# Feed-forward part of a two-stage layer: Newton steps of the norms on GpSimd, norms in pieces, a shared last tile, a halved last block

## Chip, cores and metric

The kernel runs on one core of one Trainium2 chip, in float32. The metric is the device time of one execution in microseconds. The time before is the median of three runs.

## What is computed

A layer of two parts on `x` with 4 sequences of 1024 tokens and 256 features (T = 4096 rows):

```python
x = x + layernorm(attn(layernorm(x)))     # gated delta rule, 32 value heads, chunks of 64
x = x + layernorm(ffn(layernorm(x)))
def ffn(x):                               # weights are lut[idx], 16 entries
    h = silu(x @ lut[gate_idx].T) * (x @ lut[up_idx].T)     # 688 wide
    return h @ lut[down_idx].T
def layernorm(x):
    return (x - mean(x)) / sqrt(var(x) + 1e-5)
```

## The kernel before

The main part (attention) takes the first 4200 us. It is one unrolled loop over 64 units of work on all engines, and it also builds the feed-forward weights from the table: for each of 16 slices of `WC` = 268 columns, VectorE compares the indices with each of the 16 entries (L896) and GpSimd adds up the results (L1438); the slices go to DRAM as `wtd`. A barrier (L1875 to L1897) ends it. A is then the sum of the attention's output, in SBUF.

The feed-forward part has five functions, one for each engine's queue: `ffn_sp`, `ffn_dve`, `ffn_pe`, `ffn_act`, and after the change `ffn_pool`. The order of the work on an engine is the order in which its function writes it, and semaphores hold the engines together. It goes in 8 blocks `b` of 512 tokens (4 rows of tiles of 128 tokens, `js`).

- **Norms (VectorE).** Three norms for each block: norm 0 of the attention's output, added to x (L1619, result in A); norm 1 of that, into xs, as input of the matmuls; norm 2 of the feed-forward output F, added to A (L1640). Each is `stats` (4 bn_stats, 4 bn_aggr, the variance, and `newton` for 1/sqrt: a seed and 3 rounds of 4 small instructions, L97 to L106) and `norm_out` (4 instructions, L1575).
- **Tiles of the hidden width.** 688 = 5 x 128 + 48, so FT = 6 tiles t. `gate_up(b, t)` on TensorE (L1667) has a group of matmuls for gate and one for up, into two PSUM banks: strip and emit for even t, ml and mr for odd t. Weights are stationary, 512 tokens move; the last tile has 48 weight columns. ScalarE takes silu of gate (`sg`, L1712), VectorE multiplies it with up (`gate`, L1602, result in hb).
- **Down.** `down(b, n)` for 4 groups n of 128 tokens (L1677), two into bank kv, two into bank qa; ScalarE copies them to F (`fo`, L1716).
- **TensorE's order** in a block b: gate_up 0, 1, 2; down(b-1) 0, 1 (kv); gate_up 3, 4, 5; transposes of xs for block b+1 (pp, L1655); down(b-1) 2, 3 (qa). gate_up(b, t) waits until the multiply two tiles earlier is done (`s["h"]` at i-1 with i = 6b + t), because that frees its banks; down waits for all six of its block.
- **VectorE's order** in step j (block b = j-1): gate 0; stats and out of norm 0 of block j; gate 1; the add; gate 2; stats and out of norm 1 of block j; gate 3, 4; stats of norm 2 of block j-2, which waits for its F; gate 5; out and add of norm 2.

Of the kernel before, what the change touches and what calls it, by code (L numbers as in the profile page):

```python
# [8 lines left out]
I32 = mybir.dt.int32  # L9
ALU = mybir.AluOpType  # L10
# [1547 lines left out]
def norm_stats(nc, dv, s, st, mv, var, rstd, tn, src, j, k):

    v = nc.vector  # L1560
    js = slice(4 * j, 4 * j + 4)
    for n in range(4):
        v.bn_stats(st[:, 4 * j + n, :], src[:, 4 * j + n, :]).then_inc(s["bs"], 1)  # L1563
    for n in range(4):
        dv.wait_ge(s["bs"], NT + 4 * k + n + 1)
        v.bn_aggr(mv[:, 4 * j + n, :], st[:, 4 * j + n, :]).then_inc(s["mv"], 1)  # L1566
    dv.wait_ge(s["mv"], NT + 4 * k + 4)
    v.tensor_scalar(var[:, js], mv[:, js, 1], 1e-5, None, ALU.add).then_inc(s["rsq"], 1)
    newton(dv, s["rsq"], 14 * (k + 2) + 1, var[:, js], rstd[:, js], tn[:, js])
    dv.wait_ge(s["rsq"], 14 * (k + 3))  # L1570


def norm_out(nc, s, mv, rstd, src, fin, j):
    for n in range(4 * j, 4 * j + 4):
        nc.vector.tensor_scalar(fin[:, n, :], src[:, n, :], mv[:, n, 0:1], rstd[:, n:n + 1],  # L1575
                                ALU.subtract, ALU.mult).then_inc(s["xn"], 1)


def norms_before(i, j):

    if i < 2:
        return 2 * j + i + max(0, j - 2)
    return 2 * min(j + 3, 8) + j


def ffn_dve(nc, s, g, f, bk):
    dv, v = Engine(nc.vector), nc.vector

    def stats(i, j, src):
        norm_stats(nc, dv, s, f.st[:, i], f.mv[:, i], f.var[:, i], f.rstd[:, i], f.tn[:, i], src, j,  # L1590
                   norms_before(i, j))

    def out(i, j, src, fin):
        norm_out(nc, s, f.mv[:, i], f.rstd[:, i], src, fin, j)

    def gate(b, t):
        i = b * FT + t
        rows = 128 if t < FT - 1 else FR
        dv.wait_ge(s["sg"], i + 1)
        dv.wait_ge(s["gu"], 2 * i + 2)  # L1600
        dv.wait_ge(s["dp"], 4 * (b - 1))
        v.tensor_tensor(f.hb[b % 2][0:rows, t, :], bk.all[3 + 2 * (i % 2)][0:rows, :], f.sg[i % 2][0:rows, :],  # L1602
                        ALU.mult).then_inc(s["h"], 1)

    for j in range(10):
        gates = [(j - 1, t) for t in range(FT)] if 1 <= j <= 8 else []
        if gates:
            gate(j - 1, 0)
        if j < 8:
            js = slice(4 * j, 4 * j + 4)  # L1610
            if j < 4:
                dv.wait_ge(s["da%d" % (j // 2)], 16)
            stats(0, j, f.A)
            out(0, j, f.A, f.A)
            if gates:
                gate(j - 1, 1)
            dv.wait_ge(s["xn"], NT + 4 * norms_before(0, j) + 4)
            dv.wait_ge(s[f"x{j // 2}"], 32)
            v.tensor_tensor(f.A[:, js, :], f.A[:, js, :], f.xs[:, js, :], ALU.add).then_inc(s["x1f"], 1)  # L1619
            if gates:  # L1620
                gate(j - 1, 2)
            dv.wait_ge(s["x1f"], j + 1)
            stats(1, j, f.A)
            out(1, j, f.A, f.xs)
        elif gates:
            gate(j - 1, 1)
            gate(j - 1, 2)
        if gates:
            gate(j - 1, 3)
            gate(j - 1, 4)  # L1630
        if j >= 2:
            b = j - 2
            js = slice(4 * b, 4 * b + 4)
            dv.wait_ge(s["fo"], 2 * b + 2)
            stats(2, b, f.F)
            if gates:
                gate(j - 1, 5)
            out(2, b, f.F, f.F)
            dv.wait_ge(s["xn"], NT + 4 * norms_before(2, b) + 4)
            v.tensor_tensor(f.F[:, js, :], f.F[:, js, :], f.A[:, js, :], ALU.add).then_inc(s["o"], 1)  # L1640
        elif gates:
            gate(j - 1, 5)
# [125 lines left out]


def program(nc, x, wqkv, wz, wo, convw, wba, dtb, alog, normw, lut, widx,  # L1770
            c_f32, c_mask, c_reset, c_u0, out):
    with ExitStack() as ctx:
# [104 lines left out]
        with ExitStack() as tmp:  # L1877
            f = Bag()
            f.A = g.A
            f.xnT = alloc(tmp, "fxnT", [128, 2, T])  # L1880
# [4 lines left out]
            f.var = alloc(tmp, "var2", [128, 3, NT])
            f.rstd = alloc(tmp, "rstd2", [128, 3, NT])
            f.tn = alloc(tmp, "tn2", [128, 3, NT])
# [3 lines left out]
            f.gu = f.ws[:, 0:4 * INTER].rearrange("p (w h n) -> p w h n", w=2, h=2)  # L1891
            f.dn = f.ws[:, 4 * INTER:].rearrange("p (t n) -> p t n", t=FT)
# [69 lines left out]
```

## Time and profile before

| | us |
|---|---|
| median of 3 runs | 4530.6 (4528.2 to 4533.37) |
| profiled execution | 4533.44 |
| its span | 4531.0 |
| main part, to the barrier | about 4201 |
| feed-forward part | about 330 |
| mean granted TensorE clock | 0.985 |

The profile shows one execution. PE is TensorE, DVE VectorE, ACT ScalarE, POOL GpSimd, SP the queue that issues most transfers. A line number is that of the code above; Newton instructions have the lines of their helper. In a timeline, equal instructions in a row are merged, xcount of them, and an idle time ahead of them stands in brackets with what ended it. Matmuls of float32 show two records each.

### The profile page before, as it was taken

Reading aid. Unit: us, or ns where it says so; the run is one execution under the profiler, and the core shown is the slowest. Engines: PE = TensorE matmul, PEld = TensorE weight load, DVE = VectorE, ACT = ScalarE, POOL = GpSimd, SP = SyncE. Lnnn points to the kernel's source line nnn. Section 1 sums busy time; section 2 is a strip of 40 time slices with the busy share of each in tenths; the row PEclk is TensorE's granted clock in tenths of the full one; section 3 lists DMA queues with packets and bytes.
Section 4 is the critical chain, followed back from the end, with each engine's and each line's share of the span. In section 5 each row is a group of like instructions: output and inputs, shape, how many; then the busy total and the mean of one; then the engine's idle time right before and its main releaser. Section 6 shows DMA issues by size and latency. Waiting matters only on the chain. (4 is left out here: it accounts for less than half of the span.)

```text
span 4531.0 us, 93023 instructions
## 1 busy us (share of the span) xinstructions
PE 4297.6 (95%) x30676; PEld 3229.5 (71%) x30676; DVE 3523.2 (78%) x8064; ACT 2981.9 (66%) x6124; POOL 2987.7 (66%) x8711
## 2 busy tenths in 40 slices
PE   5899999999999999999999999999999999998898
PEld 2577777777777777777777777777777777776444
DVE  6688888888888888878888788878888888885554
ACT  3577777777777767766777767766777767774111
POOL 1677777777777777777777777777777777774000
PEclk7899999999999999999999999999999999999899
DMA  4222222222222222222222222222232222210200
GB/s 133 56 65 60 67 67 46 67 59 68 67 57 65 60 67 59 55 71 64 67 67 55 64 63 59 62 68 60 67 75 47 69 58 69 64 36 20 71 14 19
DMA packets 592240, 275.17 MB, mean 61 GB/s; under 512 B 464400, under 2 KB 548880, under 8 KB 582544
## 3 DMA queue, kind: packets, MB, share of 16 engines
q1 hardware_dynamic: 591040, 266.62, 23.9%
q8 instruction: 244, 4.00, 0.4%
q0 software_dynamic: 720, 2.62, 0.3%
q14 instruction: 236, 1.93, 0.1%
HBM read 221.84 MB, written 47.28 MB: 59 GB/s over the span
## 5 line engine op out<-in xcount | busy, mean ns | idle before, releaser
L714 DVE SCALAR_TENSOR_TENSOR CV<-pp,CW,CV 128x1023 f32<-128x1023 f32 (+2 forms) x768 | 980.3, 1276 | 33.1 <-ACT CV L1076 21.8
L339 PE MATMUL pp<-A,W 128*128 128x512 f32 x2048 | 970.4, 602 | 30.1 <-DVE CV L714 18.8
L1373 POOL TENSOR_TENSOR UL<-UL,TM 128x126 f32<-128x126 f32 (+22 forms) x1984 | 743.4, 375 | 155.4
L1370 POOL TENSOR_TENSOR TM<-UL,XL 128x126 f32<-128x126 f32 (+22 forms) x1984 | 708.5, 357 | 147.2 <-issue 12.6
L339 PEld LDWEIGHTS pp<-A,W 128*128 128x128 f32 x2048 | 377.7, 193 | 338.8 <-issue 307.2
L1172 ACT ACTIVATE QE<-qa,TAB 128x128 f32<-128x128 f32 x1024 | 318.2, 362 | 407.9 <-PE qa L468 407.8
L834 DVE SCALAR_TENSOR_TENSOR St<-St,TAB,kv 128x128 f32<-128x128 f32 x1024 | 309.0, 343 | 325.0 <-PE kv L487 317.2
L1183 ACT ACTIVATE VS<-qa,EB 128x128 f32<-128x128 f32 x1024 | 319.1, 364 | 300.5 <-PE qa L478 294.7
L510 PE MATMUL emit<-Wz,A 128*128 128x256 f32 x2048 | 492.0, 383 | 4.3 <-DVE A L885 4.1
L531 PE MATMUL emit<-Wo,NTr 128*128 128x256 f32 x2048 | 493.7, 384 | 1.3 <-ACT NTr L1216 1.3
L1076 ACT ACTIVATE CV<-pp,CW 128x1024 f32<-128x1024 f32 x256 | 285.0, 1113 | 231.2 <-PE pp L339 231.2
L531 PEld LDWEIGHTS emit<-Wo,NTr 128*128 128x128 f32 x2048 | 375.9, 191 | 55.2 <-ACT NTr L1216 11.2
L510 PEld LDWEIGHTS emit<-Wz,A 128*128 128x128 f32 x2048 | 370.0, 191 | 48.0 <-DVE A L885 5.8
L820 DVE SCALAR_TENSOR_TENSOR R<-kv,TAB,V 128x128 f32<-128x128 f32 x1024 | 309.9, 344 | 119.0 <-PE kv L458 112.8
L478 PEld LDWEIGHTS qa<-R,N 128*128 128x128 f32 x2048 | 299.1, 191 | 140.7 <-issue 122.5
L458 PE MATMUL kv<-St,QK 128*128 128x256 f32 x1024 | 336.2, 410 | 43.5 <-DVE St L834 43.0
L871 DVE SCALAR_TENSOR_TENSOR CO<-CO,ty,emit 128x128 f32<-128x128 f32 x1024 | 286.9, 343 | 102.3 <-POOL ty L1357 96.5
L478 PE MATMUL qa<-R,N 128*128 128x128 f32 x2048 | 317.9, 278 | 24.7 <-issue 18.9
L487 PE MATMUL kv<-VS,K 128*128 128x256 f32 x1024 | 326.8, 401 | 5.8 <-ACT VS L1183 5.7
L1135 ACT ACTIVATE GB<-GB,AB 128x128 f32<-128x128 f32 x1024 | 328.6, 398 | 2.3
L748 DVE SCALAR_TENSOR_TENSOR X<-strip,RHO,GB 128x256 f32<-128x256 f32 x512 | 223.9, 479 | 135.7 <-ACT GB L1135 130.8
L497 PEld LDWEIGHTS qa<-VN,AT 128*128 128x128 f32 x2048 | 304.6, 191 | 23.3
(220 smaller groups left out, 9242.3 us busy)
## 6 DMA issues: line engine op xcount, KB each, us to landing
GB<-gcd SPq DMA_DIRECT2D x64, 1024.0 KB, 4.9
W<-wqkv SPq DMA_DIRECT2D x256, 128.0 KB, 3.7
XL<-xb SPq DMA_DIRECT2D x128, 256.0 KB, 3.9
UL<-c_u SPq DMA_DIRECT2D x64, 256.0 KB, 2.9
xb<-X SPq DMA_DIRECT2D x512, 32.0 KB, 1.7
Wz<-wz SPq DMA_DIRECT2D x64, 256.0 KB, 2.8
ub<-UL SPq DMA_DIRECT2D x128, 128.0 KB, 2.9
N<-ub SPq DMA_DIRECT2D x256, 64.0 KB, 2.3
```

Of the source, the lines that this page charges most:

```text
L339: ins = t.matmul(bk.pp[:, 512 * h:512 * h + 512], m.W[:, c, k, :], m.xnT[:, w // KH % 2, c, 512 * h:512 * h + 512], start=c == 0, stop=c == 1)
L458: t.matmul(bk.kv[:, 0:256], m.QK[:, 3 + w % 3, c * 128:(c + 1) * 128], sf, start=True, stop=True).then_inc(s["ks"], 1)
L478: ins = t.matmul(bk.qa[:, 256 + 128 * r:384 + 128 * r], m.N1[w % 2][:, 2 * c + r, :], m.R[k % 2][:, r, :], start=True, stop=True)
L487: t.matmul(bk.kv[:, 0:256], m.K[w % 3][:, c, :], m.VS[:].rearrange("p r d -> p (r d)"), start=True, stop=True).then_inc(s["sup"], 1)
L510: ins = t.matmul(bk.out[:, c * 256:(c + 1) * 256], m.xnT[:, w // KH % 2, h, t0:t0 + 128], m.Wz[:, w % 2, h, :], start=h == 0, stop=h == 1)
L531: ins = t.matmul(bk.out[:, c * 256:(c + 1) * 256], m.NTr[:, 2 * c + r, :], m.Wo[:, w % 2, r, :], start=r == 0, stop=r == 1)
L714: v.scalar_tensor_tensor(m.CV[:, t, d:S], bk.pp[:, 0:S - d], m.CW[:, w % KH, t, 3 - d:4 - d], m.CV[:, t, d:S], ALU.mult, ALU.add).then_inc ...
L1135: ins = a.activation(row, row, ACT.Exp, bias=m.AB[w % 2][:, 2 * q + c, r:r + 1])
L1172: ins = a.activation(m.QE[:, r, :], bk.qa[:, r * 128:(r + 1) * 128], ACT.Copy, scale=m.TAB[w % 2][:, EG, c, r:r + 1])
L1183: ins = a.activation(m.VS[:, r, :], bk.qa[:, 256 + r * 128:384 + r * 128], ACT.Copy, scale=m.EB[w % 2][:, c, r:r + 1])
L1370: gp.tensor_tensor(m.TM[:, 0:a, 0:b], m.UL[:, 0:a, k:k + 1].to_broadcast([128, a, b]), m.XL[:, k, k + 1:32].unsqueeze(1).to_broadcast([128 ...
L1373: gp.tensor_tensor(m.UL[:, 0:a, k + 1:32], m.UL[:, 0:a, k + 1:32], m.TM[:, 0:a, 0:b], ALU.subtract).then_inc(s["sub"], 1)
```

## The change

The Newton rounds of all norms go from VectorE to GpSimd (`newton_pool` with 12 small instructions, as the main part has it), but for the last block's norm 2; VectorE still computes the seed. VectorE's order is written anew: norms 0 and 1 are two blocks ahead of the gates, `stats`, `out` with its add, and the second norm stand between different gates, and norm 2 of a block is spread over the block two later. Gate and up of the last tile share one group of matmuls with 112 weight columns (48 gate, 16 zero, 48 up), one PSUM bank, partitions 0 to 47 and 64 to 111; down then contracts over all 128 rows of the last tile, of which GpSimd has set the unused ones to zero. In the diff, s1(j) is `stats(0, j)`, o1(j) `out(0, j)` with the add of x; s2, o2 are norm 1; s3(b), o3(b) norm 2 of block b; root(i, j) on GpSimd waits for the seed of norm i, block j, and runs `newton_pool`. The last block's norm 2 is worked off by `last(k)` in two halves of 2 x 128 tokens, with `newton` on VectorE, and so is its transfer. WC grows from 268 to 270.

```diff
-FR = INTER - 128 * (FT - 1)
-WCOLS = 4 * INTER + FT * HID
+FM = 128 * (FT - 1)
+FR = INTER - FM
+HC = 2 * FM + 64 + FR
+GUC = 2 * HC
+WCOLS = GUC + FT * HID
...
 def ffn_dve(nc, s, g, f, bk):
...
     def stats(i, j, src):
-        norm_stats(nc, dv, s, f.st[:, i], f.mv[:, i], f.var[:, i], f.rstd[:, i], f.tn[:, i], src, j,
-                   norms_before(i, j))
+        js = slice(4 * j, 4 * j + 4)
+        for n in range(4 * j, 4 * j + 4):
+            v.bn_stats(f.st[:, i, n, :], src[:, n, :]).then_inc(s[f"nb{i}"], 1)
+        dv.wait_ge(s[f"nb{i}"], 4 * j + 4)
+        for n in range(4 * j, 4 * j + 4):
+            v.bn_aggr(f.mv[:, i, n, :], f.st[:, i, n, :]).then_inc(s[f"nm{i}"], 1)
+        dv.wait_ge(s[f"nm{i}"], 4 * j + 4)
+        v.tensor_scalar(f.var[:, i, js], f.mv[:, i, js, 1], 1e-5, None, ALU.add).then_inc(s[f"nv{i}"], 1)
+        dv.wait_ge(s[f"nv{i}"], 2 * j + 1)
+        v.tensor_scalar(f.rstd[:, i, js].bitcast(I32), f.var[:, i, js].bitcast(I32), -0.5, MAGIC, ALU.mult,
+                        ALU.add).then_inc(s[f"nv{i}"], 1)
     def out(i, j, src, fin):
+        dv.wait_ge(s[f"np{i}"], 12 * j + 12)
+        for n in range(4 * j, 4 * j + 4):
+            v.tensor_scalar(fin[:, n, :], src[:, n, :], f.mv[:, i, n, 0:1], f.rstd[:, i, n:n + 1],
+                            ALU.subtract, ALU.mult).then_inc(s[f"nx{i}"], 1)
+...
     def gate(b, t):
+        dv.wait_ge(s["gu"], GUN * b + min(2 * t + 2, GUN))
...
+            dv.wait_ge(s["hz"], 2)
+            v.tensor_tensor(f.hb[b % 2][64:64 + FR, t, :], bk.all[2 + 2 * (i % 2)][64:64 + FR, :],
+                            f.sg[i % 2][64:64 + FR, :], ALU.mult).then_inc(s["h"], 1)
+    def last(k):
+        n0, i0 = NT - 4 + 2 * k, 15 * k
+        js = slice(n0, n0 + 2)
+        dv.wait_ge(s["fo"], 15 + k)
...
+        newton(dv, s["nl"], 14 * k + 1, f.var[:, 2, js], f.rstd[:, 2, js], f.tn[:, js])
...
+    s1(0)
+    s1(1)
+    o1(0)
+    s2(0)
+    o1(1)
+    s2(1)
+    o2(0)
+    o2(1)
+    for b in range(8):
+        gate(b, 0)
+        if b < 6:
+            s1(b + 2)
+        gate(b, 1)
+        if b >= 2:
+            s3(b - 2)
+        gate(b, 2)
+        if b < 6:
+            o1(b + 2)
+            s2(b + 2)
+        gate(b, 3)
+        if b >= 2:
+            o3(b - 2)
+        gate(b, 4)
+        if b < 6:
+            o2(b + 2)
+        gate(b, 5)
+    s3(6)
+    o3(6)
+    last(0)
+    last(1)
+def ffn_pool(nc, s, f):
+    for hb in f.hb:
+        gp.memset(hb[:, FT - 1, :], 0.0).then_inc(s["hz"], 1)
+    root(0, 0)
+    root(0, 1)
+    root(1, 0)
+    root(1, 1)
+    for b in range(8):
+        if b < 6:
+            root(0, b + 2)
+        if b >= 2:
+            root(2, b - 2)
+        if b < 6:
+            root(1, b + 2)
+    root(2, 6)
...
     def gate_up(b, t):
+        if t == FT - 1:
+            for h in range(2):
+                ins = nc.tensor.matmul(bk.all[2 + 2 * (i % 2)][0:64 + FR, :], f.gu[:, h, 2 * FM:HC],
+                                       f.xnT[:, h, b * 512:(b + 1) * 512], start=h == 0, stop=h == 1)
+            ins.then_inc(s["gu"], 1)
+            return
...
     def down(b, n):
...
-                                   f.hb[b % 2][0:rows, t, n * 128:(n + 1) * 128], f.dn[0:rows, t, :],
+                                   f.hb[b % 2][:, t, n * 128:(n + 1) * 128], f.dn[:, t, :],
```

## Rows read from the trace of the kernel before

**Rows 1.** Page, section 1: busy us, share of the span, instructions.
```profile
PE 4297.6 (95%) x30676; PEld 3229.5 (71%) x30676; DVE 3523.2 (78%) x8064; ACT 2981.9 (66%) x6124; POOL 2987.7 (66%) x8711
```

**Rows 2.** Windows between the blocks' first matmuls: length, engines' busy us, clock, DMA share.
```profile
core 0: us, PE busy (x) PEld busy (x) DVE busy (x) ACT busy (x) POOL busy (x), PEclk, DMA share, GB/s
4242.90:4276.60 33.70, 33.65 (x104) 17.69 (x104) 14.97 (x58) 5.27 (x9) 0.00 (x0) 1.00 0.00 0
4276.60:4312.80 36.20, 33.92 (x105) 17.61 (x104) 21.97 (x86) 5.87 (x10) 0.00 (x0) 1.00 0.05 15
4312.80:4350.80 38.00, 35.71 (x105) 18.20 (x105) 22.08 (x86) 5.87 (x10) 0.00 (x0) 0.96 0.04 14
...
4462.80:4500.00 37.20, 34.92 (x97) 17.36 (x96) 10.56 (x33) 4.78 (x8) 0.00 (x0) 0.95 0.04 14
```

**Rows 3.** Waits, 4250 to 4531 us: us in total, times, longest.
```profile
PE ml L1667 <- DVE hb L1602: 13.7, 6, 2.3
```

**Rows 4.** Timeline of PE, blocks 1 to 3: start, us, what, [idle before].
```profile
4282.61 1.98 PE L1667 MATMUL ml<-fxnT,ws 128*128 128x512 f32 x4 [2.28 <-DVE hb L1602]
...
4302.51 1.92 PE L1667 MATMUL ml<-fxnT,ws 128*48 128x512 f32 x4
4304.26 1.88 PE L1667 MATMUL mr<-fxnT,ws 128*48 128x512 f32 x4
...
4318.85 3.68 PE L1667 MATMUL ml<-fxnT,ws 128*128 128x512 f32 x4 [2.29 <-DVE hb L1602]
```

**Rows 5.** Timeline of DVE, block 6.
```profile
4463.62 1.41 DVE L1563 BATCH_NORM_STATS2 st<-F 128x6 f32<-128x256 f32 x4 [10.22 <-ACT F L1716]
...
4465.54 0.17 DVE L97 TENSOR_SCALAR rstd<-var 128x4 int32<-128x4 int32 x1
...
4468.13 0.68 DVE L1602 TENSOR_TENSOR hb<-mr,sg 48x512 f32<-48x512 f32 x1
4468.73 1.36 DVE L1575 TENSOR_SCALAR F<-F,mv,rstd 128x256 f32<-128x256 f32 x4
```

**Rows 6.** Timelines of DVE (first row) and PE at the start of the part.
```profile
4201.78 1.41 DVE L1563 BATCH_NORM_STATS2 st<-A 128x6 f32<-128x256 f32 x4 [0.33 <-PEq L1875]
...
4214.27 1.97 PE L1655 MATMUL pp<-cf,xs 128*128 128x128 f32 x8 [13.54 <-DVE xs L1575]
4217.02 3.42 PE L1667 MATMUL strip<-fxnT,ws 128*128 128x512 f32 x4 [0.78 <-ACT fxnT L1704]
...
4229.41 1.98 PE L1667 MATMUL ml<-fxnT,ws 128*128 128x512 f32 x4 [0.39 <-DVE hb L1602]
...
4237.55 1.92 PE L1667 MATMUL ml<-fxnT,ws 128*48 128x512 f32 x4 [1.00 <-DVE hb L1602]
```

**Rows 7.** GpSimd: timelines of POOL and DVE, and one Newton line (ns min/median/max).
```profile
36.22 1.80 POOL L1442 MEMSET N<- 128x2048 f32 x1 [35.78 <-PE kv L546]
...
68.92 1.13 POOL L1355 TENSOR_SCALAR tk<-tk 128x8 f32<-128x8 f32 x1
...
68.78 2.35 DVE L757 TENSOR_TENSOR GB<-GB,cm 128x1024 f32<-128x1024 f32 x2
...
L1355 POOL TENSOR_SCALAR tk<-tk x192: 195/203/1131, 67.8 to 4071.9; 128x8 f32<-128x8 f32 x192
...
4190.70 0.16 DVE L861 TENSOR_SCALAR ty<-tv 128x4 int32<-128x4 int32 x1
4194.34 1.12 DVE L871 SCALAR_TENSOR_TENSOR CO<-CO,ty,emit 128x128 f32<-128x128 f32 x4 [3.47 <-POOL ty L1357]
```

**Rows 8.** Timelines of PE (first row) and DVE at the end.
```profile
4505.96 8.06 PE L1677 MATMUL kv<-ws,hb 128*128 128x256 f32 x24 [5.91 <-DVE hb L1602]
...
4520.66 1.41 DVE L1563 BATCH_NORM_STATS2 st<-F 128x6 f32<-128x256 f32 x4 [12.20 <-ACT F L1716]
...
4526.58 1.23 DVE L1640 TENSOR_TENSOR F<-F,A 128x1024 f32<-128x1024 f32 x1
```

**Rows 9.** One line's durations (ns min/median/max), and DMA issues (KB, us to landing).
```profile
L1438 POOL TENSOR_TENSOR wd<-wd,wv x240: 748/755/761, 98.6 to 4098.3; 128x268 f32<-128x268 f32 x120
...
y<-F SPq DMA_DIRECT2D x8, 512.0 KB, 2.9
```

More of the change, by code:

```diff
@@ L22 @@
 FT = (INTER + 127) // 128
-FR = INTER - 128 * (FT - 1)
-WCOLS = 4 * INTER + FT * HID
+FM = 128 * (FT - 1)
[3 more added lines that the diff above has]
+WCOLS = GUC + FT * HID
 WC = WCOLS // KH
-GUK = -(-4 * INTER // WC)
+GUK = -(-GUC // WC)
+GUN = 2 * FT - 1
 MAGIC = 1597463007.0
@@ L1555, in main_pool @@
     return start, loop
[L1558 to L1583, printed above, removed]
 def ffn_dve(nc, s, g, f, bk):
@@ new lines, in s1, with o1, s2, o2 @@
+    def s1(j):
+        if j < 4:
+            dv.wait_ge(s["da%d" % (j // 2)], 16)
+        stats(0, j, f.A)
+    def o1(j):
+        js = slice(4 * j, 4 * j + 4)
+        out(0, j, f.A, f.A)
+        dv.wait_ge(s["nx0"], 4 * j + 4)
+        dv.wait_ge(s[f"x{j // 2}"], 32)
+        v.tensor_tensor(f.A[:, js, :], f.A[:, js, :], f.xs[:, js, :], ALU.add).then_inc(s["x1f"], 1)
+    def s2(j):
+        dv.wait_ge(s["x1f"], j + 1)
+        stats(1, j, f.A)
+    def o2(j):
+        out(1, j, f.A, f.xs)
@@ L1596, in gate, with s3, o3 @@
+    def s3(b):
+        dv.wait_ge(s["fo"], 2 * b + 2)
+        stats(2, b, f.F)
+    def o3(b):
+        js = slice(4 * b, 4 * b + 4)
+        out(2, b, f.F, f.F)
+        dv.wait_ge(s["nx2"], 4 * b + 4)
+        v.tensor_tensor(f.F[:, js, :], f.F[:, js, :], f.A[:, js, :], ALU.add).then_inc(s["o"], 1)
     def gate(b, t):
         i = b * FT + t
-        rows = 128 if t < FT - 1 else FR
         dv.wait_ge(s["sg"], i + 1)
-        dv.wait_ge(s["gu"], 2 * i + 2)
+        dv.wait_ge(s["gu"], GUN * b + min(2 * t + 2, GUN))
@@ L1601, in gate @@
         dv.wait_ge(s["dp"], 4 * (b - 1))
[L1602 to L1642, printed above, removed]
@@ new lines, in gate @@
+        if t < FT - 1:
+            v.tensor_tensor(f.hb[b % 2][:, t, :], bk.all[3 + 2 * (i % 2)][:, :], f.sg[i % 2][:, :],
+                            ALU.mult).then_inc(s["h"], 1)
+        else:
+            dv.wait_ge(s["hz"], 2)
[5 more added lines that the diff above has]
+        dv.wait_ge(s["fo"], 15 + k)
+        for n in range(n0, n0 + 2):
+            v.bn_stats(f.st[:, 2, n, :], f.F[:, n, :]).then_inc(s["nb2"], 1)
+        dv.wait_ge(s["nb2"], n0 + 2)
+        for n in range(n0, n0 + 2):
+            v.bn_aggr(f.mv[:, 2, n, :], f.st[:, 2, n, :]).then_inc(s["nm2"], 1)
+        dv.wait_ge(s["nm2"], n0 + 2)
+        v.tensor_scalar(f.var[:, 2, js], f.mv[:, 2, js, 1], 1e-5, None, ALU.add).then_inc(s["nl"], 1)
+        newton(dv, s["nl"], 14 * k + 1, f.var[:, 2, js], f.rstd[:, 2, js], f.tn[:, js])
+        dv.wait_ge(s["nl"], 14 * k + 14)
+        for n in range(n0, n0 + 2):
+            v.tensor_scalar(f.F[:, n, :], f.F[:, n, :], f.mv[:, 2, n, 0:1], f.rstd[:, 2, n:n + 1],
+                            ALU.subtract, ALU.mult).then_inc(s["nx2"], 1)
+        dv.wait_ge(s["nx2"], n0 + 2)
+        v.tensor_tensor(f.F[:, js, :], f.F[:, js, :], f.A[:, js, :], ALU.add).then_inc(s["o"], 1)
@@ new lines, in ffn_dve, with root @@
+    last(1)
+def ffn_pool(nc, s, f):
+    po, gp = Engine(nc.gpsimd), nc.gpsimd
+    def root(i, j):
+        js = slice(4 * j, 4 * j + 4)
+        po.wait_ge(s[f"nv{i}"], 2 * j + 2)
+        newton_pool(po, s[f"np{i}"], 12 * j, f.var[:, i, js], f.rstd[:, i, js], f.tp[:, i, js])
+    for hb in f.hb:
[12 more added lines that the diff above has]
+    root(2, 6)
@@ L1660, in gate_up @@
         i = b * FT + t
-        rows = 128 if t < FT - 1 else FR
         pe.wait_ge(s["ws"], 16)
@@ L1664, in gate_up @@
         pe.wait_ge(s["h"], i - 1)
+        if t == FT - 1:
[4 more added lines that the diff above has]
+            return
         for w in range(2):
             for h in range(2):
-                ins = nc.tensor.matmul(bk.all[2 + 2 * (i % 2) + w][0:rows, :], f.gu[:, w, h, t * 128:t * 128 + rows],
+                ins = nc.tensor.matmul(bk.all[2 + 2 * (i % 2) + w][:, :], f.gu[:, h, w * FM + t * 128:w * FM + t * 128 + 128],
                                        f.xnT[:, h, b * 512:(b + 1) * 512], start=h == 0, stop=h == 1)
@@ L1675, in down @@
         for t in range(FT):
-            rows = 128 if t < FT - 1 else FR
             ins = nc.tensor.matmul(bk.all[6 + n // 2][:, (n % 2) * 256:(n % 2) * 256 + 256],
-                                   f.hb[b % 2][0:rows, t, n * 128:(n + 1) * 128], f.dn[0:rows, t, :],
+                                   f.hb[b % 2][:, t, n * 128:(n + 1) * 128], f.dn[:, t, :],
                                    start=t == 0, stop=t == FT - 1)
@@ L1708, in sg @@
         i = b * FT + t
-        rows = 128 if t < FT - 1 else FR
-        ac.wait_ge(s["gu"], 2 * i + 1)
+        ac.wait_ge(s["gu"], GUN * b + min(2 * t + 1, GUN))
         ac.wait_ge(s["h"], i - 1)
-        a.activation(f.sg[i % 2][0:rows, :], bk.all[2 + 2 * (i % 2)][0:rows, :], ACT.Silu).then_inc(s["sg"], 1)
+        if t < FT - 1:
+            a.activation(f.sg[i % 2][:, :], bk.all[2 + 2 * (i % 2)][:, :], ACT.Silu).then_inc(s["sg"], 1)
+        else:
+            a.activation(f.sg[i % 2][64:64 + FR, :], bk.all[2 + 2 * (i % 2)][0:FR, :], ACT.Silu).then_inc(s["sg"], 1)
     def fo(b, k):
@@ L1751, in ffn_sp @@
     xs(3)
-    for b in range(8):
+    for b in range(9):
         sp.wait_ge(s["o"], b + 1)
-        nc.sync.dma_start(dr.out.rearrange("(n p) h -> p n h", p=128)[:, 4 * b:4 * b + 4, :],
-                          f.F[:, 4 * b:4 * b + 4, :]).then_inc(s["out"], 16)
-    sp.wait_ge(s["out"], 128)
+        ns = slice(4 * b, 4 * b + 4) if b < 7 else slice(14 + 2 * b, 16 + 2 * b)
+        nc.sync.dma_start(dr.out.rearrange("(n p) h -> p n h", p=128)[:, ns, :], f.F[:, ns, :]).then_inc(s["out"], 16)
+    sp.wait_ge(s["out"], 144)
 SEMS = ("cf", "x0", "x1", "x2", "x3", "cb", "wb", "l127", "hd", "al", "reset", "xnw", "g3a", "tabw",
@@ L1886, in program @@
             f.rstd = alloc(tmp, "rstd2", [128, 3, NT])
-            f.tn = alloc(tmp, "tn2", [128, 3, NT])
+            f.tn = alloc(tmp, "tn2", [128, NT])
+            f.tp = alloc(tmp, "tp2", [128, 3, NT])
             f.ws = alloc(tmp, "ws", [128, WCOLS])
@@ L1890, in program @@
             f.sg = [alloc(tmp, f"sg{i}", [128, 512]) for i in range(2)]
[L1891 to L1892 removed]
+            f.gu = f.ws[:, 0:GUC].rearrange("p (h n) -> p h n", h=2)
+            f.dn = f.ws[:, GUC:].rearrange("p (t n) -> p t n", t=FT)
             ffn_sp(nc, s, f, dr)
@@ L1896, in program @@
             ffn_act(nc, s, g, f, bk)
+            ffn_pool(nc, s, f)
             nc.all_engine_barrier()
@@ L1931 @@
     ba = np.stack([a["L0_attn_W_b"], a["L0_attn_W_a"]]).reshape(2, 32, 2, 128).transpose(3, 2, 0, 1)
-    gu = [a[n].reshape(INTER, 2, 128).transpose(2, 1, 0).reshape(128, 2 * INTER)
-          for n in ("L0_ffn_gate_idx", "L0_ffn_up_idx")]
-    dt = a["L0_ffn_down_idx"].T
-    dt = np.concatenate([dt, dt[:FT * 128 - INTER]], 0).reshape(FT, 128, HID).transpose(1, 0, 2).reshape(128, FT * HID)
-    wi = np.concatenate(gu + [dt], 1).reshape(128, KH, WC).transpose(1, 0, 2)
+    gi, ui = (a[n].reshape(INTER, 2, 128).transpose(2, 1, 0) for n in ("L0_ffn_gate_idx", "L0_ffn_up_idx"))
+    gu = np.zeros((128, 2, HC), gi.dtype)
+    gu[:, :, 0:FM], gu[:, :, FM:2 * FM] = gi[:, :, 0:FM], ui[:, :, 0:FM]
+    gu[:, :, 2 * FM:2 * FM + FR], gu[:, :, 2 * FM + 64:HC] = gi[:, :, FM:], ui[:, :, FM:]
+    di = a["L0_ffn_down_idx"].T
+    dt = np.zeros((FT * 128, HID), di.dtype)
+    dt[0:FM], dt[FM + 64:FM + 64 + FR] = di[0:FM], di[FM:]
+    dt = dt.reshape(FT, 128, HID).transpose(1, 0, 2).reshape(128, FT * HID)
+    wi = np.concatenate([gu.reshape(128, GUC), dt], 1).reshape(128, KH, WC).transpose(1, 0, 2)
     cf, mask, reset, u0 = consts()
```

3 lines of the change are left out of this document (1 added, 2 removed), and 3 rows, old and new, of the table SEMS.

## The prediction, made before the changed kernel ran

> **What bounds the kernel now.** I read the page first, then the windows, then the waits, then the timeline of each engine around the waits. TensorE is busy 95% of the span [rows 1], so a change is worth what it takes from TensorE's work or from TensorE's idle time. The change touches only the feed-forward part, which begins where VectorE reads A after the barrier (4201.78 us), so I cut the windows at the first matmul of each block b, the one of gate_up(b, 0) [rows 2]. Block 1 (4242.9 to 4276.6) has PE busy for 33.65 of 33.70 us: that is a block with no wait. Blocks 2 to 6 take 36.2 or 37.9 us with the same matmuls. The list of waits names the reason: TensorE waits six times, 13.7 us in all, for hb on the ml bank [rows 3], and once, 5.91 us, ahead of the last down-projection [rows 8]. In the timeline [rows 4] the first pause is at gate_up(b, 1), 2.28 us, whose bank is freed by gate(b-1, 5). In the next such place (block 6) VectorE runs that multiply at 4468.13, though its tile was computed before the block began, since the `stats(2, ...)` of the third norm stands ahead of it: this waits 10.22 us for the F of the last down-projection, starts at 4463.62 and takes 4.5 us, of which 13 Newton instructions are 2.6 [rows 5]. The pause of 5.91 us is the same multiply again [rows 8].
>
> **The start.** Today VectorE needs 12.5 us from 4201.78 until TensorE's first transpose at 4214.27 [rows 6]. The new order puts more ahead of it. A `stats` up to the seed's start takes 4465.54 - 4463.62 = 1.92 us and the seed 0.2, so 2.1 without Newton steps; an `out` is 1.4 [rows 5], the add 1.23 [rows 8]. A chain on GpSimd is 12 instructions spaced 0.28 us: from VectorE's seed at 4190.70 to its next reader at 4194.34 it is 3.64 us, so 3.4 from GpSimd's first to VectorE's next [rows 7]. From zero: s1(0) to 2.1, s1(1) to 4.25; GpSimd has chain (0,0) from 2.2 to 5.6; o1(0) 5.6 to 8.2; s2(0) to 10.35; o1(1), whose chain ended at 9.0, to 13.0; s2(1) to 15.15, while chain (1,0) ends at 13.7; o2(0) at 15.15, the transpose 0.79 later: 15.95. The two memsets ahead of the chains are 512 columns each; 2048 took 1.80 us [rows 7], and GpSimd has 2.2 us for them. I add 0.1 to 0.2 for what follows, so the start costs **+3.6**.
>
> GpSimd and VectorE disturb each other: a Newton instruction with a median of 203 ns took 1131 ns at 68.92 us, while VectorE ran two adds of 128x1024 [rows 7]. One chain of each tensor meets such an add of 1.22 us in the start, which lets it end at 10.2 and 15.1 instead of 9.0 and 13.9, each just before it is read (10.35, 15.15). The Trainium skill, page "SBUF — State Buffer", section "Who interferes with whom", says that a VectorE instruction with two SBUF inputs contends with a GpSimd instruction that reads SBUF, and that the second to issue fully blocks until the first has finished; the rows agree. By that rule the start would be up to 0.3 us longer than without it, and bn_stats, with one SBUF input, would not disturb GpSimd.
>
> **Block 0.** Today 25.93 us from its first matmul to block 1's. VectorE's order costs pauses of 0.39 and 1.00 us [rows 6] and a refill of about 0.16 behind each, my estimate from a group of 1.98 behind a pause [rows 4] against 1.82 to 1.88. In the new order gate(0,3) is done 18.1 us after the first matmul, when t5 could start at 18.7. The last tile is the next term: gate and up of 48 columns are two groups today, the second 4304.26 - 4302.51 = 1.75 us behind the first. A group with 48 weight columns takes as long as one with 128 (1.92 against 1.98 behind a pause) [rows 4], so one with 112 will too: one group saved, **1.75 us a block**. Block 0: -1.7 - 1.75 = **-3.45**. Start and block 0 cancel: block 1 begins near 4243 again.
>
> **Blocks 1 to 6.** From block 1's first matmul to block 7's it is 4462.8 - 4242.9 = 219.9 us [rows 2]. No pause stays if each multiply is done in time. From a block's start, with 33.7 - 1.75 = 31.95 us of matmuls: gate0 4.5; s1 to 6.6; gate1 7.9; s3 to 10.0 (its F is there since 0.7); gate2 11.3; o1 and its add to 14.0; s2 to 16.1; gate3 when t3 ends, 20.5; o3 to 23.2; gate4 23.9; o2 to 25.3; gate5 26.4. TensorE needs gate5 at 35.4: 9 us to spare. GpSimd has chain s1 from 6.4 to 9.9 (read at 11.3), s3 to 13.3 or, lengthened by o1's add, 14.5 (read at 20.5), s2 from 16.0 to 19.4 (read at 23.9). So 6 x 31.95 = 191.6, **-28.3**. Of this 10.5 is the shared tile; the rest is the pauses, 2.55 each, and the clock: after the pause at 4318.85 the ml group took 3.68 instead of 1.98 [rows 4], a loss of 1.7 in each of the four blocks of 37.9 and 37.2 us, whose mean granted clock is 0.95 or 0.96: a stretch behind the pause at 1.2 instead of 2.4 GHz [rows 2]. With no pause ahead I expect 1.00 throughout, as in block 1.
>
> **Block 7 and the last down-projection.** Block 7 takes 37.2 to the end of its last group at 4505.96 - 5.91 = 4500.05; less 2.55, 1.69 and 1.75 it is 31.2, **-6.0**. Then TensorE waits 5.9 us for gate(7,5) and restarts slowly, kv 8.06 us [rows 8] for the 5.9 that 24 such matmuls take at full clock elsewhere in the timeline; the new gate(7,5) runs before that point: **-8.05**. Behind it, with D the end of down(6): s3(6) is the new next-late thing. F at D+0.7, seed D+2.7, chain to D+6.3, o3(6) to D+8.95. F of the first half has been ready since D+6.65, so it waits 2.3 us. A half costs, from the durations of the whole [rows 5, 8]: stats 0.75, aggregate 0.25, var 0.2, 13 Newton instructions 2.6, out 0.75, add 0.65: 5.2. Two run one after the other: D+19.35, where today's tail at full clock would be D+19.7: **-0.4**, not the 2.0 that half the elementwise work would suggest. The last transfer halves (landing at 2.9 us [rows 9]; between no gain and 1 us): I take **-0.3**.
>
> **The main part** does the same instructions, with 270 columns instead of 268 for building the weights. 240 adds on GpSimd at 755 ns [rows 9], 0.75% longer, are 1.4 us beside TensorE, VectorE's steps for them less; bounds -3 to +4, taken at 0. Extra last-tile rows in `down` cost nothing: a matmul's time follows its 256 columns; zero rows only fill it. ScalarE's and VectorE's last tile keep 512 columns.
>
> **Sum:** 3.6 - 3.45 - 28.3 - 6.0 - 8.05 - 0.4 - 0.3 = -42.9. Span 4531.0 to 4488.1; the profiled run was 4533.44, so 4490.5 for it. The median of the three runs is 4530.6, which gives **4488** (4487.7).
>
> **Rivals.**
> (1) Newton chains twice as long. The instruction of 1131 ns speaks for it, the median of 203 ns over 192 of its kind against it [rows 7]. The blocks don't notice (o2 would start at 26.8, gate5 28.9, needed at 35.4), but the start has three chains in a row (+7.4) and the tail one (+3.4): 4499. Chance 0.08.
> (2) Slower: one mechanism, GpSimd's instructions held by VectorE at 1.1 us each, as the longest row, so 13.2 us a chain. Three chains a block are then 39.6 us, more than TensorE's 31.95, and GpSimd sets the pace: 7 x 7.65 = 54, the start 29, the tail 10, together +93 on 4488: 4581. It becomes slower than before from about 0.93 us an instruction on. Against it: VectorE's two-input adds cover only 2.5 us of a block. Chance 0.02.
> (3) The last tile saves nothing, because a group with 112 weight columns costs what the two did: 8 x 1.75 back, 4502. The equal times of 48 and 128 columns speak against it. Chance 0.03.
> (4) The main part, 4200 us long, moves by more than 4 us, since its buffers and semaphores shift: either way, 4478 or 4500. No row speaks for it. Chance 0.10.
> (5) The pauses go but TensorE is granted 1.2 GHz somewhere else for one stretch or more, 1.7 us each, or some pause of the waits' kind remains: 4490 to 4497. Chance 0.12.
> The forecast case has 0.65, with a range of its own of 4484 to 4493. The range that holds 8 in 10 takes in (5), the bounds above and part of (1) and (4): 4480 to 4499. A measurement here can tell about 0.2%, 9 us. All cases but (2) and a far outlier of (4) are faster by more: faster 0.95, same 0.02, slower 0.03.
>
> **What would show it.** Right: windows of 32 us between strip's first matmuls with the clock at 1.00, no wait of TensorE for hb beyond the start, the first transpose near 4217.8, kv following qa without a gap, the end of the last F near 4485. Wrong: `o1` or `o2` waiting for GpSimd on VectorE for microseconds within a block; Newton instructions with a mean well above 0.3 us; L1667's last group above 2 us; a start of the feed-forward part that isn't at 4201.8.

## The result

The changed kernel takes 4473.9 us (median of 4 runs, 4472.6 to 4475.1) against 4531.8 us beside it: ratio 0.9875, 95% interval 0.9863 to 0.9887, or 57.9 us less. Forecast were 4488 us, in a range of 4480 to 4499. The profiled execution has a span of 4470.8 us, 60.2 less than the one of before. In a later series the same two kernels stood at 4476.3 and 4529.6 (ratio 0.9881, 0.9865 to 0.9898).

The windows of the changed kernel, cut at the same places as [rows 2]; the columns are those of [rows 2].

```profile
4196.20:4215.00 18.80, 1.99 (x9) 1.62 (x9) 14.79 (x54) 1.19 (x2) 13.02 (x50) 0.50 1.01 327
4215.00:4238.80 23.80, 22.89 (x53) 10.23 (x53) 12.80 (x38) 4.66 (x8) 4.84 (x25) 0.88 0.18 56
4238.80:4268.90 30.10, 30.10 (x100) 18.26 (x101) 12.80 (x36) 5.25 (x9) 4.73 (x24) 1.00 0.00 0
4268.90:4299.00 30.10, 30.10 (x102) 18.23 (x101) 16.65 (x50) 5.85 (x10) 8.22 (x36) 1.00 0.06 19
...
4419.60:4449.00 29.40, 29.40 (x94) 17.59 (x93) 8.70 (x21) 4.77 (x8) 2.36 (x12) 1.00 0.05 18
4449.00:4470.80 21.80, 10.36 (x49) 8.77 (x47) 13.99 (x57) 1.79 (x3) 2.36 (x12) 0.82 0.14 48
```

Blocks 1 to 7 have no pause, PE is busy in all of each window and the clock is granted at 1.00, as forecast. But a block takes 30.1 us and not 31.95: TensorE's own work is 3.6 us shorter than in the block without a pause in [rows 2], where one group of 1.75 was counted on. The timeline of PE in block 2 of the changed kernel, to be read beside [rows 4]:

```profile
4277.58 1.88 PE L1728 MATMUL emit<-fxnT,ws 128*128 128x512 f32 x4
4279.30 5.34 PE L1737 MATMUL kv<-ws,hb 128*128 128x256 f32 x24
4284.48 1.88 PE L1728 MATMUL ml<-fxnT,ws 128*128 128x512 f32 x4
...
4291.35 1.88 PE L1722 MATMUL ml<-fxnT,ws 128*112 128x512 f32 x4
4293.06 1.04 PE L1711 MATMUL pp<-cf,xs 128*128 128x128 f32 x8
4293.94 5.34 PE L1737 MATMUL qa<-ws,hb 128*128 128x256 f32 x24
```

From the start of kv to the next group it is 4284.48 - 4279.30 = 5.18 us. The same 24 records took 5.86 in the kernel before.

Each part of the feed-forward stage, in us, read from the starts of these groups in the two traces:

| part | before | after | difference | forecast |
|---|---|---|---|---|
| first norm to first transpose | 12.49 | 16.03 | +3.54 | +3.6 |
| block 0, from its first matmul | 25.93 | 23.80 | -2.13 | -3.45 |
| blocks 1 to 6 | 219.93 | 180.82 | -39.11 | -28.3 |
| block 7 to the end of qa | 37.17 | 29.40 | -7.77 | -6.0 |
| from there to VectorE's end | 27.76 | 19.35 | -8.41 | -8.45 |
| to the end of the span | 3.19 | 2.45 | -0.74 | -0.3 |
| feed-forward part, with 2.75 ahead of block 0 | 329.2 | 274.6 | -54.6 | -42.9 |
| main part (start of the first norm) | 4201.8 | 4196.2 | -5.6 | 0 |

### The profile page after: what moved, and what is told of

Same layout as the page of the kernel before. It is cut to its first block and busy times, and to the rows that moved or that the text cites. A ratio compares the mean times of both kernels' runs of the same rounds, so it can differ in the third digit from the quotient of the medians.

```text
span 4470.8 us, 92997 instructions
## 1 busy us (share of the span) xinstructions
PE 4252.6 (95%) x30644; PEld 3229.0 (72%) x30644; DVE 3483.3 (78%) x7803; ACT 2976.3 (67%) x6124; POOL 3039.3 (68%) x8989
```

## The experiments

**Why is a block shorter than forecast?** Theory A: a group of matmuls whose number of rows differs from its neighbours' costs TensorE extra. Theory B, the one of the prediction: only the columns count. Two kernels put the 48 rows back into the changed kernel, and take them out of the kernel before.

e1_down48, edit against the changed kernel:

```diff
         for t in range(FT):
+            rs = slice(0, 128) if t < FT - 1 else slice(64, 64 + FR)
...
-                                   f.hb[b % 2][:, t, n * 128:(n + 1) * 128], f.dn[:, t, :],
+                                   f.hb[b % 2][rs, t, n * 128:(n + 1) * 128], f.dn[rs, t, :],
```

> The changed kernel, but down's last tile contracts over its 48 rows (64 to 111) again instead of 128. Theory A (a group whose row count differs from its neighbours' costs TensorE extra at each change of shape): in the trace of before 24 records of down take 5.86 us from group to group, in that of after 5.18, so 0.34 for each of 32 groups n: +10.9 us, about 4485, and blocks of 31.5 us instead of 30.1. Theory B (a matmul follows its columns alone, as predicted): 0, 4474, and the missing time lies elsewhere.

e5_down128, edit against the kernel before (and the two memsets of hb's last tile on GpSimd, which the multiply waits for):

```diff
-            rows = 128 if t < FT - 1 else FR
...
-                                   f.hb[b % 2][0:rows, t, n * 128:(n + 1) * 128], f.dn[0:rows, t, :],
+                                   f.hb[b % 2][:, t, n * 128:(n + 1) * 128], f.dn[:, t, :],
```

> The kernel before, but down's last tile contracts over 128 rows, of which GpSimd has set 48 to 127 to zero; nothing else changed. Theory A: -10.9 us, about 4521, block 1 at 32.3 instead of 33.7 us. Theory B: no change, 4532. The pauses for the gate multiply stay at about 2.3 us in both.

Measured, with 4526.6 us for the kernel before beside them: e1 4480.4 us (4475.6 to 4485.2; ratio to before 0.9895, 0.9879 to 0.9912), its blocks 31.68 us, its feed-forward part 284.4. That is 9.8 more than the changed kernel's, and 10.8 more than the 273.6 of e12, the changed kernel again (below), whose block 0 took as long as e1's (22.8 us). e5 4510.8 (ratio 0.9968, 0.9955 to 0.9981), its block 1 32.22 us instead of 33.68, its feed-forward part 317.5 (-11.7), with pauses still there, of 2.48 us. Timelines of PE, block 2: e1, then e5.

```profile
4282.66 5.93 PE L1738 MATMUL kv<-ws,hb 128*128 128x256 f32 x24
```

```profile
4276.82 2.46 PE L1674 MATMUL ml<-fxnT,ws 128*128 128x512 f32 x4 [2.48 <-DVE hb L1603]
4285.49 5.34 PE L1683 MATMUL kv<-ws,hb 128*128 128x256 f32 x24
```

The duration of the 24 records goes to 5.93 with 48 rows in the new kernel and to 5.34 with 128 in the old one. Theory B falls: what 24 such records take goes with the rows of the last tile, in the new order and in the old. TensorE's weight loads show where it is lost, e1 first and then the changed kernel:

```profile
4297.97 2.03 PEld L1738 LDWEIGHTS qa<-ws,hb 128*128 128x128 f32 x10
4300.33 0.29 PEld L1738 LDWEIGHTS qa<-ws,hb 48*128 48x128 f32 x2 [0.33 <-issue]
4300.96 2.02 PEld L1738 LDWEIGHTS qa<-ws,hb 128*128 128x128 f32 x10 [0.33 <-issue]
```

```profile
4263.71 5.05 PEld L1737 LDWEIGHTS qa<-ws,hb 128*128 128x128 f32 x24
```

In e1 the weight load waits 0.33 us ahead of the first load of the other shape, on the way in and on the way out; in the changed kernel the 24 loads follow each other without a gap. Is it the change of shape, or are 48-row matmuls slow in themselves? e11_fewer_switches has as many 48-row matmuls as e1, but half as many changes of shape. What it has beyond e1's edit:

```diff
-        for t in range(FT):
+        order = [FT - 1] + list(range(FT - 1)) if n % 2 else list(range(FT))
+        for t in order:
...
-                                   start=t == 0, stop=t == FT - 1)
+                                   start=t == order[0], stop=t == order[-1])
```

> e1_down48 (down's last tile over 48 rows), but every second group n takes that tile first, so that two 48-row tiles stand next to each other and the shape changes half as often. Theory A1 (the change of shape costs): blocks of 30.9 instead of 31.68 us, half of the 1.56 comes back. Theory A2 (a matmul over 48 rows is slower in itself): 31.68 stays.

Measured in one execution (4477.7 us): blocks of 30.91 us. PEld and PE of e11:

```profile
4296.02 0.62 PEld L1739 LDWEIGHTS qa<-ws,hb 128*128 128x128 f32 x3
4296.97 0.73 PEld L1739 LDWEIGHTS qa<-ws,hb 48*128 48x128 f32 x4 [0.33 <-issue]
4298.03 2.02 PEld L1739 LDWEIGHTS qa<-ws,hb 128*128 128x128 f32 x10 [0.33 <-issue]
```

```profile
4279.69 5.74 PE L1739 MATMUL kv<-ws,hb 128*128 128x256 f32 x24
```

A block has 4 visits to the other shape in e1, 2 in e11 and none in the changed kernel: 31.68, 30.91, 30.12. Each visit costs 0.39 us (0.37 by e5's block 1 against that of before), and 48-row matmuls next to each other cost nothing more: A1. The Trainium skill, page "TensorEngine Tiling (Array Packing)", section "Key Properties", says that changing the tiling mode drains TensorE. It doesn't say that matmuls over 48 rows and over 128 rows are two modes. If they are, these runs agree with it, at 0.39 us for a change and the change back; that a drain is what costs the time isn't shown by them.

**How the gain divides.** e2_order is the changed kernel with the old last tile (`gate_up`, `sg`, `gate`, `down` and the weights' layout as before; no memset). e3_tile is the kernel before with only these pieces of the change.

> The changed kernel with the old last tile (two groups of 48 columns, down over 48 rows, 268 columns a slice): new order, Newton on GpSimd and halved last block alone. Theory A: the tile's part of the gain goes back, 8 x 1.75 for the group, 10.9 for down and 8 x 0.2 for the changes of shape around the last tile: 4474 + 26.5 = 4500. Theory B: 8 x 1.75 alone, 4488. The main part: if its 5.6 us earlier end is due to the 270 columns, VectorE's first norm is back at about 4202; if it is chance or due to something else, it stays where it is by chance.

> The kernel before with the shared last tile alone (270 columns a slice), old order, Newton on VectorE, last block whole. Theory A: 4532 - 26.5 = 4505, with the six pauses of about 2.3 us still there. Theory B: 4532 - 14 = 4518. If the 270 columns are what moves the main part, its norm starts at about 4196 and the time is 5 us less again.

Measured: e2 4494.6 us (ratio 0.9931, 0.9916 to 0.9946), feed-forward part 300.4, blocks 33.68. e3 4500.2 (ratio 0.9942, 0.9928 to 0.9957), feed-forward part 305.8. In e2's PE the blocks are just those that [rows 2] had without a pause (33.70), and no pause is left; in e3 all six pauses stand, at 2.49 us:

```profile
4262.80 1.92 PE L1714 MATMUL ml<-fxnT,ws 128*48 128x512 f32 x4
4264.56 1.88 PE L1714 MATMUL mr<-fxnT,ws 128*48 128x512 f32 x4
4266.37 1.09 PE L1702 MATMUL pp<-cf,xs 128*128 128x128 f32 x8
4267.30 5.93 PE L1724 MATMUL qa<-ws,hb 128*128 128x256 f32 x24
```

```profile
4272.11 2.46 PE L1686 MATMUL ml<-fxnT,ws 128*128 128x512 f32 x4 [2.49 <-DVE hb L1610]
...
4306.68 2.90 PE L1686 MATMUL ml<-fxnT,ws 128*128 128x512 f32 x4 [2.49 <-DVE hb L1610]
```

By the feed-forward parts, the new order with Newton on GpSimd and the halved end is worth 329.2 - 300.4 = 28.8 us, the tile on top of it 300.4 - 274.6 = 25.8; the tile alone, in the old order, 23.4. In a block the tile brings 33.68 - 30.12 = 3.56 us: 1.72 are the group saved, 1.56 the changes of shape in `down` (e1), and the rest, 0.28, those around the 48-column groups (1.76 us from the first to the second and 1.81 from that to pp, against 1.72 within a shape).

Sums of whole parts are less sharp than this. e9 (below) has the same feed-forward code as the kernel before, and its part took 332.5 us, 3.3 more: 1.6 in block 0 and 1.7 in blocks 1 to 6, where the clock fell behind four pauses instead of three. So the 28.8 could as well be 32, and 23.4 against 25.8 doesn't show that the tile brings less alone.

**What is GpSimd for?** e4_newton_dve keeps the new order and puts all Newton rounds back on VectorE (in `stats`, with `newton`; GpSimd has only the memsets).

> The changed kernel with all Newton rounds on VectorE, in the same new order. Theory: in a block VectorE has 3 x 2.4 us more, gate 3 then ends at about 22.5 us from the block's start, where TensorE wants it at 22.35, so 0 to 0.3 us a block; the start has three stats of 4.5 us and more in a row ahead of the first transpose: 24.2 instead of 16.0 us, +8.2; the end -0.8. Sum 4474 + 7.4 to 9.5 = 4481 to 4484. Rival (the move to GpSimd is what removes the pauses): pauses of 2 us come back in every block with the lower clock behind them, +20 us or more.

Measured: 4479.3 us (ratio 0.9896, 0.9881 to 0.9911), feed-forward part 285.0: +10.4. The first transpose is 24.21 us behind the first norm (24.2 expected), most blocks take 30.34 us against 30.12. No pause between the blocks comes back. Only block 0 has one, which I had not expected:

```profile
4243.52 1.97 PE L1703 MATMUL ml<-fxnT,ws 128*112 128x512 f32 x4 [1.78 <-DVE hb L1617]
```

So the rival falls: the order, in which no `stats` that waits for F stands ahead of gate 5, is enough to remove the pauses. GpSimd's part on top of it is 8.2 us at the start and 2 to 3 us in block 0 (25.87 us against 23.80, and 22.78 in e12).

The fourth case, the old order with Newton on GpSimd, was not run. There the 12 Newton instructions that stand between the seed and gate 5 [rows 5] would be gone from VectorE. They take 12 x 0.2 = 2.4 us, and the six pauses are 2.28: by this estimate the move alone could have removed these too, though of the pause of 5.91 us it would leave some 3.5. What is shown is that the order suffices, not that it is needed.

**The end: is halving worth anything?** e7_whole has the last block's third norm and its transfer in one piece:

```diff
-    last(0)
-    last(1)
+    last()
```

> The changed kernel with the last block's third norm in one piece. By the trace of after its last half begins at 4463.06, while F has been there since 4460.0: the two halves wait for each other. In one piece 7.15 us from 4460.05 on: VectorE ends 18.2 us behind the end of down(6) instead of 19.35, the transfer is 0.3 longer: -0.8 us. Rival (halving saves half of the elementwise work at the end): +2 us.

Measured: 4468.5 us (4463.0 to 4472.1; ratio 0.9868, 0.9853 to 0.9882), feed-forward part 274.0 (-0.6). VectorE ends 18.3 us behind the end of down(6), as expected, against 19.35 with halves. The timelines of VectorE at the end: the changed kernel, then e7.

```profile
4456.70 1.23 DVE L1611 TENSOR_TENSOR F<-F,A 128x1024 f32<-128x1024 f32 x1
4457.84 0.75 DVE L1631 BATCH_NORM_STATS2 st<-F 128x6 f32<-128x256 f32 x2
...
4463.06 0.74 DVE L1631 BATCH_NORM_STATS2 st<-F 128x6 f32<-128x256 f32 x2
...
4467.66 0.69 DVE L1643 TENSOR_TENSOR F<-F,A 128x512 f32<-128x512 f32 x1
```

```profile
4456.80 1.41 DVE L1630 BATCH_NORM_STATS2 st<-F 128x6 f32<-128x256 f32 x4 [2.10 <-ACT F L1776]
...
4462.85 1.22 DVE L1642 TENSOR_TENSOR F<-F,A 128x1024 f32<-128x1024 f32 x1
```

The first half doesn't start when its F is there (4454.8) but when o3(6) is done, and the second half waits for the first one's Newton steps. In one piece VectorE even idles for 2.10 us and is done earlier. The halved transfer gives back part of it: it lands after 2.1 us instead of 2.9. Of the 0.6 us this leaves 0.3 (1.05 less on VectorE, 0.78 more behind it); the other 0.3 is block 0's start, which scatters. The medians can't show so little, and they come from different series; it is the two traces that do.

**A better start?** The new order puts two blocks' norms ahead of the first transpose, at +3.54 us. e8_start_end takes block 0's norms first, with Newton on VectorE, and joins the end anew (s3(6) with Newton on VectorE, one Newton chain for both halves of the last block). The order of the start:

```diff
     s1(0)
-    s1(1)
     o1(0)
     s2(0)
+    o2(0)
+    s1(1)
     o1(1)
     s2(1)
-    o2(0)
     o2(1)
```

> The changed kernel with the start in the old order (s1(0), o1(0), s2(0), o2(0) first, their Newton rounds on VectorE) and a new end: s3(6) with Newton on VectorE, the last block's statistics in halves, one Newton chain for both, output in halves. The start costs 12.5 us instead of 16.0 to the first transpose (-3.5), and block 0's multiplies have 5 us of VectorE's norms of block 1 ahead of them, which is hidden as in before (TensorE's first gate is wanted at 5.2 us). The end: 17.5 us behind down(6) instead of 19.35 (-1.9). Sum 4474 - 5.4 = 4468.5. Rival: the 3.5 us come back, because the norms of block 1 now delay gate 0 of block 0: 4472.

e10_weave has e8's start and end, and interleaves the rest with block 0:

```diff
...
+    s1(1)
     o1(1)
+    gate(0, 0)
     s2(1)
-    o2(0)
+    gate(0, 1)
+    s1(2)
+    gate(0, 2)
     o2(1)
-    for b in range(8):
+    gate(0, 3)
+    o1(2)
+    gate(0, 4)
+    s2(2)
+    gate(0, 5)
+    for b in range(1, 8):
         gate(b, 0)
+        if b == 1:
+            o2(2)
...
```

> The start of e8_start_end (block 0's norms first, Newton on VectorE) and its end, but the norms of blocks 1 and 2 in pieces between the gates of block 0, so that gate(0,0) no longer has both norms of block 1 ahead of it. In e8_start_end TensorE waited 4.04 us for that gate and block 0 took 30.25 us for 23.8. Theory: no pause in block 0, which takes 23.5 to 25; first transpose 12.7 us behind the first norm; end 17.7 us behind down(6): feed-forward part 274.6 - 3.3 - 1.7 = 269.6 us. Rival (VectorE has too much to do in block 0, whatever the order): pauses of 1 to 3 us, 271 to 275.

> The changed kernel again, on the same chip as the two below. Its feed-forward part took 274.6 us from VectorE's first norm to the end of the span; it should do so again within 1.5 us, while the end of the main part may lie anywhere between 4190 and 4202, as in the ten traces so far. Median 4467 to 4474.

Measured: e8 4471.1 us (ratio 0.9874, 0.9858 to 0.9891), feed-forward part 276.1, 1.5 longer than the changed kernel's. The start and the end gained nearly what was expected (12.75 us to the first transpose for 12.5, VectorE's end 17.7 us behind down(6) for 17.5), but block 0 took 30.25 us: the rival was right, and cost more than the 3.5 us it said, since a pause of 4.04 us came and the clock fell again behind it. e12_after, the changed kernel on the chip of e10: 4476.3 (4472.6 to 4478.5; 0.9881, 0.9865 to 0.9898), above the 4467 to 4474 that I expected; its feed-forward part, 273.6, is as expected. e10 4469.0 (4466.0 to 4470.6; ratio 0.9863, 0.9848 to 0.9877), feed-forward part 269.6, as expected, with no wait of PE for hb left. PE in block 0, e8 and then e10:

```profile
4208.89 3.75 PE L1740 MATMUL strip<-fxnT,ws 128*128 128x512 f32 x4 [0.78 <-ACT fxnT L1776]
4212.44 2.65 PE L1740 MATMUL emit<-fxnT,ws 128*128 128x512 f32 x4
...
4222.56 3.78 PE L1740 MATMUL strip<-fxnT,ws 128*128 128x512 f32 x4 [4.04 <-DVE hb L1630]
4226.14 2.63 PE L1740 MATMUL emit<-fxnT,ws 128*128 128x512 f32 x4
```

```profile
4211.92 3.75 PE L1751 MATMUL strip<-fxnT,ws 128*128 128x512 f32 x4 [0.78 <-ACT fxnT L1787]
4215.47 2.89 PE L1751 MATMUL emit<-fxnT,ws 128*128 128x512 f32 x4
4218.19 1.88 PE L1751 MATMUL ml<-fxnT,ws 128*128 128x512 f32 x4
```

e10 is faster than both kernels: 4.0 us less than e12 in the feed-forward part and 7.3 in the medians, none of its four runs being as slow as the fastest of e12. The 3.3 us that the feed-forward part doesn't explain are no more than the main part's scatter (below).

**The main part, 5.6 us shorter.** e9_wc270 is the kernel before with the slices of 270 columns:

```diff
-WCOLS = 4 * INTER + FT * HID
+WCOLS = 4 * INTER + FT * HID + 32
```

> The kernel before with slices of 270 instead of 268 columns (32 unused columns), nothing else changed, so only the main part's buffers and the weight building differ. Theory C (the 270 columns, that is, buffers moved by 8 bytes each, make the main part 5 us shorter): norm starts near 4196 to 4198, median 4527. Theory D (chance from execution to execution, or something else): norm starts at 4199 to 4203, median 4530 to 4533.

Measured: 4525.7 us against 4527.5 beside it, ratio 0.9997 (0.9987 to 1.0006): no difference. Its one trace starts the first norm at 4190.9, earlier than any other and outside what either theory said. So one trace's start says nothing: over the thirteen traces it lies between 4190.9 and 4201.8, those with 268 columns at 4195.9, 4196.2 and 4201.8, and the one of before is the latest of all. The 5.6 us between the two first traces lie within this scatter, and nothing shows them to be an effect of the change; an effect of a few us isn't ruled out either, since e9's interval reaches 0.13% or 5.9 us below before. What makes the main part end up to 11 us apart was not looked for.

## Why the prediction was wrong

**The sign and the mechanism held.** The pauses came from gate 5 behind a `stats` that waits for F, and the new order removes them: six pauses, the one ahead of the last `down`, and the lower clock behind four of them are gone. e2 (the order with Newton on GpSimd and the halved end) shows it: of the -42.9, the tile's 8 x 1.75 = 14 taken off, -28.9 were forecast and -28.8 measured, and each part of the stage lies within 0.6 us of its term. That the sum fits to 0.1 is partly luck: block 0 missed by 0.6 one way and the last transfer by 0.5 the other, and the old kernel's own part varies by 3 us.

**The step that failed** is in the main part's paragraph: "Extra last-tile rows in `down` cost nothing: a matmul's time follows its 256 columns; zero rows only fill it." They cost less than nothing, for they spare TensorE 4 visits to another shape in each block, 0.39 us each (e1, e11), and the last tile of gate and up spares about 0.28 more than its group. Nothing in the prediction foresaw this, so the extra gain is luck. A block was put at 31.95 and is 30.12. That is 6 x 1.8 = 10.8 us in blocks 1 to 6 and 1.8 in block 7, 12.6 in all. Less the 1.3 that block 0 lost, and with 0.4 more at the end, it makes the 11.7 us by which the feed-forward part beat the forecast. The remaining 2 to 3 us of the medians lie outside the feed-forward part of the two traces and within the main part's scatter. The trace of before had signs of the step. One stands in a view that I did not read, the groups with shapes kept apart, the other in its weight loads:

```profile
L1677 PE MATMUL kv<-ws,hb 128*128 128x256 f32 x160 | 40.1, 400 | 5.9 <-DVE hb L1602 5.9
L1677 PE MATMUL kv<-ws,hb 48*128 48x256 f32 x32 | 11.1, 428 | 0.0
```

```profile
4273.02 0.29 PEld L1677 LDWEIGHTS qa<-ws,hb 48*128 48x128 f32 x2 [0.33 <-issue]
4273.65 2.02 PEld L1677 LDWEIGHTS qa<-ws,hb 128*128 128x128 f32 x10 [0.33 <-issue]
```

Columns of the first two: instructions, busy us, mean ns, idle time before. The mean of the 128-row records holds the slow ones behind the last pause, yet 48 rows are slower still; in block 1 alone, without a pause, it is 384 ns against 428. The last two are a timeline, with the same 0.33 us as in e1. Instead I took a block whose PE is busy for 33.65 of 33.70 us [rows 2] for a block in which TensorE works all the time. Its busy time held some 1.8 us of changes of shape (4 x 0.39 + 0.28).

**The start** was right: 16.03 us for 15.95 to 16.1. A GpSimd chain takes 3.3 us, and those that meet an add of VectorE are longer by one instruction of 1.18 us, twice, and end just before they are needed. VectorE at 4206.65 and 4211.45 has no wait, so the disturbance cost the start nothing:

```profile
4203.25 1.23 DVE L1594 TENSOR_TENSOR A<-A,xs 128x1024 f32<-128x1024 f32 x1
...
4206.65 1.38 DVE L1581 TENSOR_SCALAR A<-A,mv,rstd 128x256 f32<-128x256 f32 x4
...
4203.35 1.18 POOL L1355 TENSOR_TENSOR tp<-rstd 128x4 f32<-128x4 f32 x1
4204.61 0.20 POOL L1357 TENSOR_TENSOR tp<-tp,var 128x4 f32<-128x4 f32 x1
```

Rivals (1) and (2) fall: the chains have 69 instructions on each Newton line, with medians of 193 to 199 ns. Rival (3) falls with L1722: one group of 112 columns takes 1.71 us (4291.35 to 4293.06). (4) was right in that the main part's end moves by more than 4 us from trace to trace, but e9 shows no effect of moved buffers. (5) was right in nothing: the clock is 1.00 in blocks 1 to 7.

**Block 0** came out 1.3 us longer than forecast. Its pauses are gone; its first two groups took 6.40 us instead of 4.97 until the third began, at the lower granted clock (0.88 in its window). In e12, the same kernel, they took 5.38. With the code of before they took 4.97 in its own trace and 6.57 in e9's, whose block 0 took 27.51 us instead of 25.93. So this term has 1 to 1.6 us of scatter of its own, and I had assumed the value of one trace, which is the lowest of all.

**The end** is exact where it was worked out (19.35 us from the end of down(6) to VectorE's end), and rightly put as small. Its gain of 0.4 us was reckoned against the old tail of 19.7, though. The last `down` has itself become 1.5 us shorter without its changes of shape (10.5 us from kv's start to qa's end, 12.0 in e2), so in one piece the end is at 18.3, and e7 shows that halving costs 1.1 us on VectorE and gives back 0.8 with the smaller transfer. Behind VectorE's end 0.74 us went instead of 0.3.

**The range** was too narrow below. Its bounds came from the rivals that I had thought of, which all added time but for one side of (4); none was that the tile's shape saves more than its group. The main part was bounded at -3 to +4, and its traces lie 11 us apart.

## What to carry to other kernels

A busy TensorE may still lose time inside what the trace shows as busy: before taking a "full" stretch as the floor, compare means of the same operation by shape, and look for short idle times of the weight load where the shape changes. If one tile of a contraction is short, filling it with zero rows can be cheaper than leaving them out. When norms or other side work feed a pipeline on one queue, the order on that queue (nothing that waits for a late result ahead of a multiply that frees a bank) was enough here to end the pauses, and moving the Newton steps to another engine on top of it was worth 10.4 us more, nearly all at the start and in block 0. Splitting the last piece pays only if the engine is free when the first half arrives.

## What the runs showed of the hardware that I had not expected

- A change of the number of rows from 128 to 48 and back cost TensorE 0.39 us, with two records or four in between (e1, e11).
- GpSimd's small instructions are a little slower while VectorE runs `out` (128x256, with two scalars for each partition from SBUF): 0.23 to 0.36 us instead of 0.20, where adds of two SBUF inputs hold them for up to 1.18.
- The time that TensorE stays at the lower clock after an idle start differs between executions of one kernel: its first two groups took 6.40 and 5.38 us (the changed kernel and e12).
- A transfer of y of 256 KB landed after 2.1 us (the changed kernel), one of 512 KB after 2.9 (e7).
